# Two-layer graph kernel: layer 1's memory laid in zones over layer 0, its first logits issued among layer 0's last turns, row products one unit later, the mid reload split

## The reference

```python
h = x @ W;  hr = h.reshape(N, 64, 4)                       # layer 0
e = s_src[:, None, :] + s_dst[None, :, :]
e = where(e >= 0, e, -0.2 * e)
att = softmax(e * adj[:, :, None], axis=1)
out = einsum('ijh,jfh->ihf', att, hr) + bias + x @ res_w + res_b
x = layernorm(x + out)

R = (adj + I) / rowsum                                      # layer 1; S = adj
for n in range(2):
    q = Xa @ W1.T @ W2.T;  k = Xa @ W3.T
    A = softmax(q @ k.T) cut to the top 0.9 of each row's mass, rows rescaled
    Xf = R @ Xf;  Xa = A @ Xa
    Z += Xf @ U1[n].T + Xa @ U2[n].T
x = layernorm(x + layernorm(x + Z) * ln_g + ln_b)
```

## Time and profile before

| | |
|---|---|
| median of 3 runs | 3900.14 us (3897.62 to 3902.06) |
| profiled execution, own time | 3899.62 us |
| its span, first to last instruction | 3897.8 us |
| time outside the span | 1.8 us |
| busy: PE 3592.3, DVE 3558.7, ACT 3059.3 us | 92%, 91%, 78% of the span |
| layer 0 (units, up to the barrier) | 0 to 1415.8 us |
| step 0 of layer 1 | 1415.8 to about 2201 us |
| step 1 | from there to 3897.8 us |

### The profile page before, as it was taken

The page is one execution under the profiler, slowest core; times in us unless marked ns, Lnnn a source line. Parts: engine busy times, 40 slices in busy tenths (PEclk is TensorE's granted clock), DMA queues, the critical chain, the costliest instruction groups (busy, mean ns, idle before and its releaser), DMA issues.

```text
span 3897.8 us, 66233 instructions
## 1 busy us (share of the span) xinstructions
PE 3592.3 (92%) x25368; PEld 3026.4 (78%) x25368; DVE 3558.7 (91%) x6048; ACT 3059.3 (78%) x3107; POOL 1524.9 (39%) x1627
## 2 busy tenths in 40 slices
PE   8888888888888859999999989999999999999996
PEld 5777777777777747778777768888888788888885
DVE  4999999999999969999999499999999899999998
ACT  6999999999999955555555378888888788888873
POOL 0112112112112101111111155556555469999997
PEclk9999999999999979999999989999999999999998
DMA  2112112112112140000000323333333433333332
GB/s 109 52 57 84 57 57 84 57 57 84 57 57 84 57 135 15 17 17 17 20 19 19 106 87 94 99 99 99 105 105 104 130 109 112 113 115 115 116 119 69
DMA packets 155583, 302.72 MB, mean 78 GB/s; under 512 B 16635, under 2 KB 116987, under 8 KB 151011
## 3 DMA queue, kind: packets, MB, share of 16 engines
q1 hardware_dynamic: 155234, 298.22, 23.7%
HBM read 256.54 MB, written 41.62 MB: 76 GB/s over the span
## 4 chain that ended last, share of the span: by engine, by line
ACT 36%; POOL 22%; DVE 17%; PE 15%; issue 10%; DMA 1%; DVEq 0%; ACTq 0%; SPq 0%; POOLq 0%; PEldq 0%; PEld 0%
ACT b L1070 8%; ACT b L1063 7%; ACT b L1235 6%; ACT b L1236 6%; DVE b L1440 5%; DVE b L1610 3%; PE ps L796 3%; ACT b L1057 3%; DVE b L1498 3%; DVE b L1496 2%; POOL b L608 2%; POOL b L605 2%; ACT b L1216 2%; PE ps L986 2%; PE ps L845 2%
## 5 line engine op out<-in xcount | busy, mean ns | idle before, releaser
L911 PE MATMUL ps<-b 128*128 128x257 f32 x4096 | 912.8, 382 | 20.4 <-DMA b<-in_adjTb 11.0
L986 PE MATMUL ps<-b 128*128 128x257 f32 x4096 | 902.8, 380 | 0.0
L911 PEld LDWEIGHTS ps<-b 128*128 128x128 f32 x4096 | 777.7, 191 | 146.4 <-DMA b<-in_adjTb 12.3
L986 PEld LDWEIGHTS ps<-b 128*128 128x128 f32 x4096 | 771.9, 190 | 113.2 <-issue 0.8
L845 PE MATMUL ps<-cb,b 128*128 128x128 f32 x4096 | 498.4, 277 | 188.0 <-ACT b L1063 147.2
L845 PEld LDWEIGHTS ps<-cb,b 128*128 128x128 f32 x4096 | 446.6, 142 | 238.4 <-ACT b L1063 170.1
L1388 DVE SCALAR_TENSOR_TENSOR b<-b 128x4096 f32<-128x4096 f32 x128 | 566.4, 4425 | 17.4 <-ACT b L1057 13.8
L1390 DVE CUSTOM_DVE_ANT_0 b<-b 128x4096 f32<-128x4096 f32 x128 | 566.4, 4425 | 4.4
L1070 ACT ACTIVATE b<-ps 128x1024 f32<-128x1024 f32 x512 | 494.6, 1079 | 48.5 <-PE ps L845 48.5
L568 POOL TENSOR_SCALAR b<-b 128x1 f32<-128x1 f32 x128 | 75.3, 588 | 1087.9 <-DVE b L1390 1087.9
L1063 ACT ACTIVATE b<-b 128x4096 f32<-128x4096 f32 x128 | 485.3, 3791 | 0.0
(11 more groups left out here) (205 smaller groups left out, 5050.2 us busy)
## 6 DMA issues: line engine op xcount, KB each, us to landing
b<-in_adjTb SPq DMA_DIRECT2D x256, 512.0 KB, 3.7
b<-in_adj SPq DMA_DIRECT2D x32, 2048.0 KB, 8.6
h_d<-b SPq DMA_DIRECT2D x63, 128.0 KB, 1.8
b<-h_d SPq DMA_DIRECT2D x63, 128.0 KB, 2.5
b<-in_xT SPq DMA_DIRECT2D x4, 1024.0 KB, 8.6
b<-in_xT SPq DMA_DIRECT2D x32, 128.0 KB, 8.4
gx_d<-b SPq DMA_DIRECT2D x32, 128.0 KB, 1.8
X_d<-b SPq DMA_DIRECT2D x32, 128.0 KB, 8.5
```

What stands on the lines that cost most here:

```text
L911: last = mm(b[:, 0:XA], aj[:, q % AJR, e, :], xf[:, j, :], start=(j == 0), stop=(j == NT - 1))
L986: last = mm(o[:, 0:XA], at[:, q % ATR, b, :], xa[:, j, :], start=(j == 0), stop=(j == NT - 1))
```

## The change

Four things are edited.

1. **Memory.** The layer 1 tiles get one buffer as large as layer 0's (53040 columns) and are laid in zones over it: KT, qT, u1, fin, pzs over the first adjacency buffer; xf over h_s; the scores eb, maxima and small tiles over sd_s; V, at, xa, aj and others over the ub buffers. The separate tile kr is gone. What lies over a dead layer 0 tile may be written before the barrier.
2. **First logits.** The key and query loads of step 0 move ahead of the barrier, to turn NT of SP's loop. `logits(0)` is split into four `first_logits(c)` among PE's last turns, with `first_logit_ev(c)` on ACT and `cmax_part(0, c)` on DVE; the fourth needs the keys of the last two tiles, which ACT now copies before the barrier. `turn_x(30)` moves ahead of the products of unit 127 and waits until all its chunks are evacuated.
3. **Row products one unit later.** rows(r) and ev_rows(r) stand at unit 4r + 10 instead of 4r + 9.
4. **Reloads.** At step 1's start the adjacency chunks 3 to 6 are interleaved with the 8 reloads of xa, which had all stood ahead of them; in the middle of step 1 seven of y's eight chunks are issued as soon as the stores of 30 row tiles and the products of the first half are through, before SP turns to the last two row tiles' stores; the eighth follows them.

```diff
-        kr = ctx.enter_context(nc.sbuf_tensor("kr", [128, N // 2 + 256], F32))
-        b1 = ctx.enter_context(nc.sbuf_tensor("b1", [128, 50600], F32))
+        b1 = ctx.enter_context(nc.sbuf_tensor("b1", [128, 53040], F32))
...
+        over_h = Region(b1, 0, SD)
+        over_sd = Region(b1, SD, AD)
+        over_adj = Region(b1, AD, UBA)
+        over_ub = Region(b1, UBA)
...
         for u in range(NU):
-            if u % 4 == 1 and u >= 9:
-                gslot[(u - 9) // 4] = i
+            if u % 4 == 2 and u >= 10:
+                gslot[(u - 10) // 4] = i
                 i += 1
...
+                if t == NT:
+                    sp.wait_ge(s_u, 4 * (NT - 1))
+                    sp.wait_ge(s_kst, 16 * NGX)
+                    kload(0)
+                    qload(0, 0)
+                    qload(0, 1)
...
-            kload(0)
-            qload(0, 0)
-            qload(0, 1)
...
-            for q in range(NQ):
-                reload(q)
...
+            for c in range(NCH):
+                adjchunk(AJR + c)
+                for q in range(NQ // NCH * c, NQ // NCH * (c + 1)):
+                    reload(q)
             gxload(0)
-            adjpairs(-1, 0)
...
                 if HT in pairs_in(n):
+                    sp.wait_ge(g["ys"], 16 * (NT - 2))
+                    sp.wait_ge(g["R"], NT * NCH)
+                    chunked(xf, y_d, 0, NQ - 1)
                     rstore(n - 1)
                     sp.wait_ge(g["ys"], 16 * NT)
-                    sp.wait_ge(g["R"], NT * NCH)
-                    chunked(xf, y_d)
+                    chunked(xf, y_d, NQ - 1, NQ)
...
+                if u == NU - 1:
+                    turn_x(NGX)
                 pv(g0)
                 pv(g0 + 1)
...
             pv(NG0 - 2)
             pv(NG0 - 1)
-            turn_x(NGX)
+            first_logits(0)
             turn_back(NT - 1)
...
+            last_keys(NGX)
+            first_logits(1)
+            first_logits(2)
+            turn_x(NGX + 1)
+            last_keys(NGX + 1)
+            first_logits(3)
             barrier(pe, kB)
...
             ev_x(NGX)
             out_turned(NT - 1)
+            first_logit_ev(0)
             ev_y0(NT - 1)
+            first_logit_ev(1)
+            first_logit_ev(2)
             ev_x(NT - 1)
-            barrier(ac, kB)
+            ac.wait_ge(s_kt, NT - NGX)
             act(KT[64:128, (NGX - KH) * 128:], bank(6)[64:128, 0:128 * (NT - NGX)], ACT.Copy).then_inc(st[0]["kk"], 1)
...
+            first_logit_ev(3)
+            barrier(ac, kB)
...
+            cmax_part(0, 0, 1)
             post_a(NT - 1)
             post_b(NT - 1)
+            cmax_part(0, 1, 2)
+            cmax_part(0, 2, 3)
+            cmax_end(0, cmax_part(0, 3, 4))
             barrier(ve, kB)
```

More of the change, by code:

```diff
@@ L65, in gat_topp_kernel, with __init__ @@
         class Region:
-            def __init__(self, base, at=0):
+            def __init__(self, base, at=0, end=None):
                 self.base = base
                 self.at = at
+                self.end = base.shape[1] if end is None else end
             def take(self, *shape):
@@ L73, in take @@
                 self.at += n
-                assert self.at <= self.base.shape[1], self.at
+                assert self.at <= self.end, self.at
                 if len(shape) == 2:
@@ L183, in gat_topp_kernel @@
         w8 = r1.take(3, 8)
-        zE = r1.take(3)
+        u2 = r1.take(2, 256)
+        xan = r1.take(2, 256)
+        xz = r1.take(4, 128)
         prs = r1.take(2, XA)
@@ L851, in _ @@
                 g0 = u * NCH
-                if u % 4 == 1 and u >= 9:
-                    rows((u - 9) // 4)
+                if u % 4 == 2 and u >= 10:
+                    rows((u - 10) // 4)
                 if u >= 1:
@@ L864, in _, with first_logits, last_keys @@
                     turn_back(u // 4 - 1)
+            def first_logits(c):
+                g = st[0]
+                if c == 0:
+                    pe.wait_ge(g["qd"][0], 32)
+                    pe.wait_ge(g["kk"], 32)
+                if c == NL // 2 - 1:
+                    pe.wait_ge(g["kk"], 34)
+                if c >= 3:
+                    pe.wait_ge(g["el"], c - 2)
+                b = bank(2 * (c % 3), 2)
+                w = slice(c * 512, (c + 1) * 512)
+                for d in range(2):
+                    p = slice(64 * d, 64 * d + 64)
+                    last = mm(b[:, 512 * d:512 * d + 512], qT[p, 0, :], KT[p, w], start=True, stop=True)
+                last.then_inc(g["pl"], 1)
+            def last_keys(t):
+                pe.wait_ge(s_ev, xslot[t] + 1)
+                keys(t, bank(6)[:, 128 * (t - NGX):128 * (t - NGX) + 128]).then_inc(s_kt, 1)
             pv(NG0 - 2)
             pv(NG0 - 1)
-            turn_x(NGX)
+            first_logits(0)
             turn_back(NT - 1)
-            for t in range(NGX, NT):
-                if t > NGX:
-                    turn_x(t)
-                pe.wait_ge(s_ev, xslot[t] + 1)
-                pe.wait_ge(s_po, NT - 1)
-                last = keys(t, bank(6)[:, 128 * (t - NGX):128 * (t - NGX) + 128])
-                if t < NT - 1:
-                    last.then_inc(s_kt, 1)
+            last_keys(NGX)
[4 more added lines that the diff above has]
+            first_logits(3)
             barrier(pe, kB)
-            pe.wait_ge(s_one, 1)
             for s in range(2):
                 g = st[s]
-                lc = [0]
+                lc = [NL // 2 if s == 0 else 0]
                 rc = [0]
@@ L1132, in _ @@
                     linear(u + 2)
-                if u % 4 == 1 and u >= 9:
-                    ev_rows((u - 9) // 4)
+                if u % 4 == 2 and u >= 10:
+                    ev_rows((u - 10) // 4)
                 for c in range(NCH):
@@ L1628, in _ @@
                     levat[n] = el_at
[L1629 to L1631 removed]
+                if s == 1:
                     rmax(0)
```

143 lines of the change are left out of this document (80 added, 63 removed).

## The result

The changed kernel takes 3942.65 us, the kernel before 3900.44: 1.0109 times as long, 95% interval 1.0091 to 1.0126. That is 42 us slower, where I had forecast 3903 and a range that ended at 3916. Its profiled execution has a span of 3939.6 us, against 3897.8.

The account below looks back on a forecast made before the run. Before, DVE paced layer 0 at 41.5 us a group and then step 0; after, the tile's load would bound layer 0. 26.6 - 3.5 - 11.3 + 2.5 + 0 - 11.0 = +3.3 us gave 3903 us, range 3870 to 3916.

Parts of the forecast that it names:

- the +26.6 us at the L1390 of unit 124: Layer 0: DVE's multiply with the adjacency tile starts at 1380.8 instead of 1354.2 us, as the tile's load becomes the bound.
- my loop: Layer 0, one group of four units: from multiply through ev_rows, stores and tile load to the next multiply, 42.59 us.
- ACT now waits for DVE at u=0: Layer 0: ACT, with 40.4 us of work in a group of 42.6, waits for DVE at u=0.
- rival (c): Layer 0: the tile lands later than before, each 0.1 us costing 2.9; 3920 us at a landing of 9.2; chance 0.12.
- estimate of 6.8 us: Layer 0 tile load of 2 MB by the skill's formula: the loop would close in 40.8 us and nothing would wait.
- ACT's lag: End of layer 0: ACT's exponential of unit 127 starts when POOL has that unit's maximum, -3.5 us.
- First logits ahead of the barrier: Layer 0 to step 0: the first exponential starts at 1422.4 instead of 1433.71, -11.3 us, bounds -9 and -13.
- The query load: Step 0: logits(2) can start 35.3 us behind the barrier's end and DVE waits, +2.5 us, bounds +1 and +5.
- Step 1's start: PE's early chunks come sooner, but the y_d stores DVE depends on keep their time: 0, at best -4 us.
- The middle of step 1: Early reload of y lets PE start product 32 sooner: -11 us, bounds -7 and -11.7.

Follow-up runs that it names:

- half filled: Changed kernel with 16 useless transposes on PE ahead of its turn at each u=0 from unit 12 on: 3909.2 us.
- PE filled: Changed kernel with 32 useless transposes on PE ahead of its turn at each u=0 from unit 12 on: 3902.3 us.
- the move alone: Kernel before with the row products one unit later and nothing else of the change: 3953.7 us.
- tf_reload_late: a_tile_first with all eight chunks of y's reload in the middle of step 1 behind the two stores again: 3885.5 us.
- a_tile_first: Changed kernel with the next adjacency tile's load on SP ahead of the row products' three stores and the wait for ev_rows: 3872.1 us.
- b_tile_first: Kernel before with the adjacency tile's load ahead of the three stores, nothing of the change: 3897.8 us.
- a_tile_ahead_of_stores: Changed kernel with the adjacency tile's load ahead of the three stores but still behind SP's wait for ev_rows: 3897.8 us.

## Why the prediction was wrong

The mechanism that I forecast is the one that runs: the load behind the stores, DVE's wait in 29 groups, ACT waiting for POOL at u=0, the gap of ACT in u=1 gone. The term of the sum that failed is its first, the +26.6 us at the L1390 of unit 124. It measured +66.1. Here is my loop against the means of 28 groups (each row is rounded by itself):

| length, us | forecast | changed | half filled | PE filled |
|---|---|---|---|---|
| multiply of u=0 to its exponential | 5.42 | 5.46 | 5.47 | 5.47 |
| exponential of u=0 to u=1 | 10.37 | 10.93 | 10.42 | 10.39 |
| exponential of u=1 to u=2 | 9.91 | 10.50 | 10.01 | 9.89 |
| exponential of u=2 to ev_rows | 6.03 | 6.02 | 6.02 | 6.02 |
| ev_rows to first store | 0.93 | 0.81 | 0.85 | 0.85 |
| first store to tile's issue | 1.33 | 1.33 | 1.33 | 1.33 |
| tile's issue to multiply | 8.6 | 8.87 | 8.61 | 8.54 |
| sum | 42.59 | 43.94 | 42.71 | 42.50 |

**The clock, 32 us.** The two stretches between exponentials are 0.56 and 0.59 us longer than forecast, 1.15 x 28. With PE kept busy both are back at what I took, to 0.02 us. So the step that failed is "ACT now waits for DVE at u=0 (42.6 less its 40.4 of work)": I had the wait in the text and priced it at nothing, because ACT had slack. But PE stands behind ACT. Its wait of up to 1.7 us ahead of the turn grew by that of ACT, and in 24 of 28 groups its clock fell to 1.2 GHz. The turn took 5.1 to 6.6 us instead of 4.3, and ACT, which evacuates it, waited in turn. All of it lies inside the loop, so it came back as more wait, up to 5.3 us for PE. My lengths were taken from rows of the kernel before, where PE was at 2.4 GHz (granted clock 1.00) in this stretch; they were not constants. The lower clock stands in the prediction, as a bound of the first logits, but not in the loop.

The Trainium skill has a page that would have warned me: "TensorE: Matmul & The Clock Gate", section "HAM oscillation — how this bites in real kernels", tells of a matmul loop whose waits for DMA bring the clock down again in every turn of the loop. The traces here agree for 24 of 28 turns (granted clock 0.50 behind a wait of 4.19 us), with one step more: it was DVE that waited for the DMA, and the wait reached PE over POOL and ACT.

**The load, 8 us.** From the tile's issue to the multiply it took 0.27 us a group more than the 8.6 that I took, x 28 = 7.6. About half of it is a step that my sum left out: from the landing to the start of the multiply the traces of the loop show 0.14 us in the mean. The other half is that the landings' mean is 8.7 where I took a median of 8.6; their median here is 8.5. That is rival (c)'s mechanism in part, and small. Since the same length is 8.54 with PE filled and 8.64 with the move alone, scatter and effect can't be told apart here.

The Trainium skill's formula (page "DMA: Bandwidth & Descriptors", section "Anatomy of one DMA — SWDGE (gpsimd) path") is for the GpSimd path, and its estimate of 6.8 us does not fit this load on SP: no landing of a tile inside layer 0 took less than 7.5 us in any run. The medians are 8.3 to 8.6 behind the stores, 9.0 just ahead of them, and 7.9 to 8.2 well ahead of them.

The step from ev_rows to the first store (-0.12 x 28 = -3.3), the first length (+1.3), the rest of the table (-0.2) and the first tile (190.15 instead of 188.3: +1.9) make up the remainder: 32.2 + 7.6 - 3.3 + 1.3 - 0.2 + 1.9 = 39.5, which is what was missing.

The other terms:

- **ACT's lag:** -3.1, forecast -3.5. Right.
- **First logits ahead of the barrier:** -11.5, forecast -11.3. Right in size and at its place.
- **The query load:** +3.9, forecast +2.5, inside its bounds. The start was right to 0.5 us; the rest is again the clock, 5.97 us instead of 3.70 for the products behind the wait.
- **Step 1's start:** 0 to -1.6, forecast 0, at best -4. Right.
- **The middle of step 1:** -11.0, forecast -11.0. Right, and tf_reload_late shows it by itself.

All terms with the measured first one: 66.1 - 3.1 - 11.5 + 3.9 - 0.6 - 1.6 - 11.0 - 0.6 = 41.6 (41.5 before rounding). With the first at 26.6 that is +2, 3902 us; with PE filled the kernel is at 3902.3. That these two agree so well is in part luck, as the filled run's own expectation was off by 9.

The range was wrong in the same way. Its upper end came from landings up to 9.2, the only unknown that I had let vary; I bounded the lengths of the loop by nothing, since all of them had a row.

## What to carry to other kernels

In an in-order queue a load pays for every wait ahead of it. Before moving a step, look on each queue for what stands behind its semaphore; here one load moved on SP turned a loss of 42 us into a gain of 27. When a change creates a periodic wait, follow it through to TensorE even where the waiting engine has slack, and price PE's work behind it at both clock levels, since durations read from the old trace hold only at the clock at which they were read. And a loop that closes within about 1 us of the bound in a 42 us period deserves a wide range upward, because a wait inside it can feed itself: DVE's wait was 2.4 us a group with PE's clock low and 1.0 with PE filled.

## What the runs showed of the hardware

- A wait of TensorE that was handed on over three engines cost its clock. In 1164 us of layer 0 the granted clock was 0.95 with waits up to 5.3 us ahead of one turn in four, and 1.00 with waits up to 1.7. The 32 transposes of a turn (128x128, f32) took 3.7 us where nothing waited, and 5.1 to 6.6 from first to last in 24 of the 28 turns behind the long wait.
- The length of the wait did not by itself decide it. In the changed kernel four turns kept the higher clock behind waits of 3.0 to 3.4 us while others behind 3.0 to 3.4 lost it. In a_tile_first PE waited 2.6 us ahead of 16 turns, and 8 of them were slow. So the cost of such a wait is a share of the turns, not a fixed sum.
- Useless transposes in PE's wait kept its clock at 1.00 and made the kernel 40 us faster where PE stood in the loop, and changed nothing where it did not.
- A 2 MB load of one tile landed in 7.9 us (median) when it was issued well ahead of the three small stores, in 8.5 behind them, and in 9.0 right ahead of them. In the kernel before the median went from 8.6 to 7.9 (b_tile_first) when the load left the stores. That the stores themselves slow the load is my reading; no run takes them away. The landings in a_tile_first, in the changed kernel and in a_tile_ahead_of_stores:

```profile
DMA to landing us min/median/max: 7.6/7.9/9.0
```

```profile
DMA to landing us min/median/max: 7.8/8.5/10.1
```

```profile
DMA to landing us min/median/max: 8.6/9.0/10.2
```

- What stays open is why the mean from issue to multiply is 8.87 us in the changed kernel, 8.64 with the move alone and 8.54 with PE filled, with landings up to 10.1, 9.7 and 9.7. Each is one profiled execution. Times of the move alone range from 3948 to 3962 us, 14 us, where the others stay within 9; the changed kernel, with the same loop, stays within 2.2, so the loop alone does not explain that range.
